# Bringing x to token order without the matrix engine: VectorE block transposes and DMA copies in a fused state-space and feed-forward kernel

## The reference

```python
# state-space layer: d_inner 1024, 8 heads of 128, state 64, convolution over 4 positions
zxbcdt = u @ W_in.T                         # z | x, B, C | dt
xBC = silu(conv_b + sum(xp[:, k:k+l] * conv_w[:, k] for k in range(4)))
dt = softplus(dt + dt_bias);  A = -exp(A_log)
# per chunk of positions and head: L = exp(segment sums of dt*A), lower triangle
Y_diag = einsum(C, B, L, x*dt)              # inside the chunk
states = einsum(B, decay, x*dt)             # what the chunk adds to the state
Y_off  = einsum(C, state before the chunk, exp(cum))
y  = Y_diag + Y_off + x * D
yg = y * silu(z)
out = (yg * rsqrt(mean(yg*yg) + eps) * norm_w) @ W_out.T
x1 = layernorm(u + out)                     # layernorm without scale or shift
# feed-forward: W_q = clip(round(W/mean|W|), -1, 1) * mean|W|
h  = silu(x1 @ Wup_q.T) * (x1 @ Wgate_q.T)  # 2048 hidden units
x2 = layernorm(x1 + h @ Wdown_q.T)
```

## Time and profile before

| | |
|---|---|
| three timed runs, us | 1473.92, 1475.54, 1475.65; median 1475.54 |
| profiled execution, us | 1476.25, its span 1473.3 |
| granted TensorE clock | 0.995 of 2.4 GHz over the span |
| busy | PE 98%, VectorE 69%, ScalarE 58%, GpSimd 29% |
| state-space part | start to 785 us |
| first 512 tokens of the feed-forward part | 785 to 875 us |
| 56 pairs | 875 us to the end, 10.36 us each |

### The profile page before, as it was taken

How to read it: one execution, slowest core, us unless ns; L and a number is a source line. 1 busy time by engine, 2 the same in 40 slices (tenths; PEclk the granted TensorE clock), 3 DMA queues, 4 the chain that set the end, 5 groups by cost and what they waited for, 6 DMA issues and landing times.

```text
span 1473.3 us, 26856 instructions
## 1 busy us (share of the span) xinstructions
PE 1444.9 (98%) x10132; PEld 1300.4 (88%) x10132; DVE 1021.8 (69%) x2223; ACT 857.7 (58%) x1651; POOL 430.6 (29%) x540
## 2 busy tenths in 40 slices
PE   8999999999999999999998999999999999999997
PEld 8889898889898898988977889999999999999996
DVE  6876686667766776677668987766665666666555
ACT  7877667676765766766762234545445454545443
POOL 5334454445435453454362106500000000000000
PEclk9999999999999999999999999999999999999999
DMA  7113312332233232322247333545353545445341
GB/s 272 65 58 87 101 59 73 87 101 86 65 96 87 83 91 57 101 88 59 87 136 253 110 110 128 167 139 161 108 179 101 158 129 162 134 127 163 94 136 65
DMA packets 141760, 168.05 MB, mean 114 GB/s; under 512 B 76480, under 2 KB 85184, under 8 KB 141632
## 3 DMA queue, kind: packets, MB, share of 16 engines
q1 hardware_dynamic: 141632, 166.35, 36.8%
HBM read 132.62 MB, written 33.69 MB: 113 GB/s over the span
## 4 chain that ended last, share of the span: by engine, by line
PE 86%; DMA 4%; DVE 4%; ACT 2%; issue 2%; SPq 1%; POOL 0%; POOLq 0%; DVEq 0%; ACTq 0%
PE ps L403 25%; PE ps L265 21%; PE ps L473 16%; PE ps L359 11%; PE ps L393 3%; PE ps L313 3%; DMA x_scratch<-s_rr 3%; PE ps L321 2%; PE ps L330 1%; PE ps L300 1%; DVE s_xact L827 1%; SPq L1376 1%; DMA s_bcx<-ct_scratch 1%; PE ps L233 1%; DVE s_rr L974 0%
## 5 line engine op out<-in xcount | busy, mean ns | idle before, releaser
L403 PE MATMUL ps<-s_xoh,s_S 128*128 128x256 f32 x896 | 220.4, 282 | 0.1
L403 PE MATMUL ps<-s_xol,s_S 128*128 128x256 f32 x896 | 220.3, 282 | 0.0
L473 PE MATMUL ps<-s_tern,s_hl 128*128 128x512 f32 x504 | 199.2, 395 | 0.0
L473 PE MATMUL ps<-s_tern,s_hh 128*128 128x512 f32 x504 | 199.2, 395 | 0.0
L265 PE MATMUL ps<-s_uhi,s_whi 128*128 128x256 f32 x1088 | 179.8, 287 | 3.0 <-ACT s_uhi L543 3.0
L403 PEld LDWEIGHTS ps<-s_xoh,s_S 128*128 128x128 f32 x896 | 169.5, 189 | 5.9 <-issue 0.8
L265 PE MATMUL ps<-s_ulo,s_whi 128*128 128x256 f32 x1088 | 173.6, 282 | 0.3 <-DVE s_ulo L812 0.3
L403 PEld LDWEIGHTS ps<-s_xol,s_S 128*128 128x128 f32 x896 | 169.5, 189 | 4.8
L265 PE MATMUL ps<-s_uhi,s_wlo 128*128 128x256 f32 x1088 | 173.5, 282 | 0.0
L1267 POOL TENSOR_TENSOR s_lnb<-s_lnb,s_cst 128x1 f32<-128x1 f32 x32 | 18.9, 595 | 501.2 <-DVE s_lnb L1115 501.2
L403 PE MATMUL ps<-s_xol,s_tern 128*128 128x256 f32 x672 | 163.7, 281 | 0.0
(11 more groups left out here) (178 smaller groups left out, 2985.8 us busy)
## 6 DMA issues: line engine op xcount, KB each, us to landing
s_S<-wsum_scratch SPq DMA_DIRECT2D x48, 512.0 KB, 3.6
s_S<-wsum_scratch SPq DMA_DIRECT2D x96, 256.0 KB, 3.4
s_bcx<-ct_scratch SPq DMA_DIRECT2D x32, 512.0 KB, 3.8
s_wst<-in_wffn SPq DMA_DIRECT2D x48, 256.0 KB, 2.8
s_wraw<-in_wffn SPq DMA_DIRECT2D x16, 768.0 KB, 7.8
s_uraw<-in_uT SPq DMA_DIRECT2D x16, 512.0 KB, 6.2
s_rr<-in_un SPq DMA_DIRECT2D x32, 256.0 KB, 3.1
x_scratch<-s_rr SPq DMA_DIRECT2D x32, 256.0 KB, 2.2
```

The source lines that it names most:

```text
L403: o = e.matmul(bank[:, 256 * mi:256 * mi + 256], wt(mi, k), xo[g % 2][:, x, k, :], start=(first and mi == 0 and k == 0 and xo is xoh), sto ...
L473: o = e.matmul(DB[c][:], y[:, 128 * c:128 * c + 128], tern[:, j, 1024:1536], start=(j == 0 and lo == 0), stop=(j == 15 and lo == 1))
```

## The change

What it does:

- `TR` and `f_xTe` are gone, and with them 256 instructions on PE and 64 on ScalarE. `f_xtr(n, k)` on VectorE transposes each block of 32 x 32 of an x tile in place in `xact`, one instruction of [128, 2, 256] a tile, 64 in all.
- `load_xT(c)` on SP's queue moves the blocks to their places: 16 DMAs a chunk, each from 32 partitions of `xact` to 32 partitions of `xT`, 8 heads by 32 numbers, so pieces of 128 B. 512 such DMAs in all.
- Y, `f_xw` and `f_xe` of the next group wait for these DMAs (`xT_landed`). `B0` is now Y's alone.
- `f_x1` moves from VectorE to ScalarE, as scale and bias of one activation; GpSimd's `f_rs1` computes the bias in a second instruction on one column.
- Only chunks 0 to 11 are transposed by `f_xt` and stored by `store_xt` in the state-space part. For chunks 12 to 31 x1 is read back from DRAM (`load_xr`), transposed (`f_xt2`) and stored (`store_xt2`) in the pairs Q of the feed-forward part, one chunk in each odd Q below 40.
- The lists that set the order are written anew on all engines, also those that say which engine splits which weight tile at the start.

```diff
-        def TR(c, half):
-            n = c // 2
-            w.wait_ge(s_silc, 5 * n + 5)
-            if c % 2:
-                w.wait_ge(s_xTe[half], c)
-            elif c:
-                w.wait_ge(s_gate[half], c)
-            for i in range(4):
-                o = e.transpose(B0[half][:, 128 * i:128 * i + 128],
-                                xact[:, 4 * half + i, 128 * (c % 2):128 * (c % 2) + 128], ident)
-            o.then_inc(s_TR[half], 1)
...
+    def xT_landed(w, c):
+        w.wait_ge(d_xT[c % 3], 256 * (c // 3 + 1))
...
         def Y(c):
             w.wait_ge(s_DI, c + 1)
-            later = c + 1 if c % 2 else c + 2
+            xT_landed(w, c)
             for half in range(2):
-                w.wait_ge(s_xTe[half], later)
-                if c % 2:
-                    w.wait_ge(s_gate[half], c)
+                w.wait_ge(s_gate[half], c)
...
# ScalarE: f_xe(n, k), the first writer of xact
-                w.wait_ge(s_TR[0], 2 * n)
-                w.wait_ge(s_TR[1], 2 * n)
+                for c in range(2 * n - 2, 2 * n):
+                    if c >= 0:
+                        xT_landed(w, c)
...
-        def f_xTe(c, half):
-            w.wait_ge(s_TR[half], c + 1)
-            if c >= 3:
-                w.wait_ge(s_Y, c - 2)
-                w.wait_ge(s_xw, c - 2)
-            e.activation(xT[:, c % 3, 4 * half:4 * half + 4, :].rearrange("p h s -> p (h s)"),
-                         B0[half][:], AF.Copy).then_inc(s_xTe[half], 1)
...
+        def f_x1(c):
+            v, r = lnb[:, c % 2, :], rr[:, c % 3, :]
+            w.wait_ge(s_rs1, 2 * c + 2)
+            e.activation(r, r, AF.Identity, scale=v[:, 11:12], bias=v[:, 12:13]).then_inc(s_x1, 1)
...
# VectorE
+        def f_xtr(n, k):
+            w.wait_ge(s_silc, 5 * n + k + 1)
+            x = xact[:, 2 * k - 2:2 * k, 0:256]
+            e.transpose(x, x).then_inc(s_xtr, 1)
...
-        def f_x1(c):
-            v, r = lnb[:, c % 2, :], rr[:, c % 3, :]
-            w.wait_ge(s_rs1, c + 1)
-            e.tensor_scalar(r, r, v[:, 8:9], v[:, 11:12], sub, mult).then_inc(s_x1, 1)
...
+        def f_xt2(c):
+            w.wait_ge(d_xs, 80 * (c - 12) + 16)
+            e.transpose(xtt[:], xtt[:]).then_inc(s_xt, 1)
...
# GpSimd: f_rs1(c)
+            w.wait_ge(s_rs1, 2 * c + 1)
+            e.tensor_scalar(v[:, 12:13], v[:, 8:9], v[:, 11:12], -1.0, mult, mult).then_inc(s_rs1, 1)
...
# SyncE
+        def load_xT(c):
+            w.wait_ge(s_xtr, 4 * (c // 2) + 4)
+            if c >= 3:
+                w.wait_ge(s_Y, c - 2)
+                w.wait_ge(s_xw, c - 2)
+            for i in range(4):
+                t = 128 * (c % 2) + 32 * i
+                for j in range(4):
+                    e.dma_start(xT[32 * i:32 * i + 32, c % 3, :, 32 * j:32 * j + 32],
+                                xact[32 * j:32 * j + 32, :, t:t + 32]).then_inc(d_xT[c % 3], 16)
...
+        def load_xr(c):
+            x1_stored(w, c)
...
+            e.dma_start(xtt[:], x1d[128 * c:128 * c + 128, :]).then_inc(d_xs, 16)
...
# SyncE, one line of the order of a period, before and after
-            load_bc(c + 3); load_wst(3 * n + 3); store_xt(c - 1); load_r0(c + 1); load_wst(3 * n + 4); load_bc(c + 4)
+            store_x1(c - 1); load_wst(3 * n + 2); load_bc(c + 3); load_xT(c + 2); load_r0(c + 1); load_wst(3 * n + 3)
```

More of the change, by code:

```diff
@@ L182, in build_program @@
     U1_AT = 4
[L183 to L187, removed]
+    DVE_LO = [16, 9, 13, 15, 12]
+    WHI_ORDER = [16, 8, 9, 10, 11, 13, 15, 12, 0, 14, 2, 6, 7, 1, 3, 5, 4]
+    POOL_LO = [8, 10, 11, 2, 14, 0, 1, 5, 6, 4, 3, 7]
+    WOHI_ORDER = [2, 3, 0, 1, 7, 4, 5, 6]
+    WOLO_ORDER = [1, 2, 4, 0, 3, 5, 6, 7]
     IP_TILES = [[16], [8, 9], [10, 11], [12, 13], [14, 15], [0, 1], [2, 3], [4, 5], [6, 7]]
@@ L210, in build_program, with x1_count @@
     XQ = ((X11, 0, 0), (D3, 0, 1), (X21, 1, 0), (X22, 1, 1))
+    def xT_landed(w, c):
+        w.wait_ge(d_xT[c % 3], 256 * (c // 3 + 1))
+    def x1_count(c):
+        return sum(80 if i < 12 else 16 for i in range(c % 3, c + 1, 3))
     def x1_stored(w, c):
-        w.wait_ge(d_x1[c % 3], 80 * (c // 3 + 1))
+        w.wait_ge(d_x1[c % 3], x1_count(c))
     def program_pe(e):
@@ L507, in program_pe @@
-        expert(10, 1); down(7); expert(11, 0); expert(11, 1); expert(12, 0); expert(12, 1); down(8); expert(13, 0)
-        expert(13, 1); expert(14, 0); down(9); expert(14, 1); down(10); expert(15, 0); expert(15, 1); down(11)
+        expert(2, 0); expert(2, 1); SQ(c + 1); OP(c + 1); expert(3, 0); expert(3, 1); expert(4, 0); down(0)
+        expert(4, 1); down(1); expert(5, 0); expert(5, 1); down(2); expert(6, 0); expert(6, 1); expert(7, 0)
+        expert(7, 1); down(3); expert(8, 0); down(4); expert(8, 1); expert(9, 0); down(5); down(6); expert(9, 1)
@@ L510, in program_pe @@
+        expert(10, 0); down(7); expert(10, 1); expert(11, 0); down(8); expert(11, 1); expert(12, 0); expert(12, 1)
+        down(9); down(10); expert(13, 0); expert(13, 1); expert(14, 0); expert(14, 1); down(11); expert(15, 0)
+        expert(15, 1)
         for Q in range(56):
@@ L1138, in program_dve @@
+            f_taps(n + 1, 4); f_dd(c + 4); f_GM(n + 1)
+            if m == NG // 2 - 1:
+                wtot()
+            f_xtr(n + 1, 1); f_xtr(n + 1, 2)
+            if m <= 3:
+                f_xt(c)
+            if m == NG // 2 - 1:
+                f_wz(c + 4)
+            f_ms(c + 2); f_gate(c + 3, 0); f_gate(c + 3, 1); f_r1(c + 2); f_sqsum(c + 3); f_xtr(n + 1, 3)
+            f_xtr(n + 1, 4); f_S(c + 3)
             if m < NG // 2 - 1:
@@ L1166, in program_dve @@
                 f_h21(Q - 1); f_h12(Q - 1)
+            if Q % 2 == 1 and Q < 40:
+                f_xt2(12 + Q // 2)
             if p == 2:
@@ L1393, in load_xt @@
             X, kh, h = XQ[i]
-            for c in range(4 * g, 4 * g + 4):
-                x1_stored(w, c)
+            if g < 3:
+                for c in range(4 * g, 4 * g + 4):
+                    x1_stored(w, c)
+            else:
+                w.wait_ge(d_xs, 80 * (4 * g + 2 * h - 10))
             if g == 1:
@@ L1476, in program_sp @@
             e.dma_start(wolr[:, k, :], wout[:, k, :]).then_inc(d_wo[k], 16)
[L1477 to L1478 removed]
+        load_xT(0); load_xT(1); load_wst(2); load_bc(2); load_r0(0); load_bc(3); load_u(3); load_wst(3); load_r0(1)
+        load_xT(2); load_wst(4); store_x1(0); load_xT(3); load_wst(5); store_ct(1); load_wst(6)
         for m in range(1, NG // 2):
             n, c = 2 * m, 4 * m - 2
[L1482 to L1487 removed]
+            load_r0(c); load_bc(c + 2); load_wst(3 * n + 1)
+            if m <= 3:
+                store_xt(c - 2)
+            store_x1(c - 1); load_wst(3 * n + 2); load_bc(c + 3); load_xT(c + 2); load_r0(c + 1); load_wst(3 * n + 3)
+            load_xT(c + 3)
+            if m <= 3:
+                store_xt(c - 1)
+            load_bc(c + 4); load_r0(c + 2); load_bc(c + 5); load_wst(3 * n + 4); load_wst(3 * n + 5)
+            if m < NG // 2 - 1:
+                load_u(n + 2)
+            store_x1(c)
+            if m < NG // 2 - 1:
+                load_u(n + 3)
+            store_x1(c + 1)
+            if m <= 3:
+                store_xt(c)
+            load_xT(c + 4); load_xT(c + 5); store_x1(c + 2)
+            if m <= 3:
+                store_xt(c + 1)
+            if m == NG // 2 - 1:
+                load_xt0()
@@ L1507, in program_sp @@
                 load_xt(g + 1, p - 1)
+            if Q % 2 == 0 and 0 < Q <= 40:
+                store_xt2(11 + Q // 2)
             if Q >= 8:
                 load_ws4(Q)
+            if Q % 2 == 0 and Q < 40:
+                load_xr(12 + Q // 2)
             if p == (4 if g == 1 else 3):
```

194 lines of the change are left out of this document (95 added, 99 removed).

## The result

The changed kernel takes 1529.12 us (median of 4 runs, 1526.45 to 1534.65) against 1475.6: a ratio of 1.0366, 95% interval 1.0332 to 1.0400. It is slower by 53.5 us, where 12 us faster was forecast, and 35 us above the end of the range. A ratio leaves out an execution that ran at a much lower clock throughout; there was one, of e8 (1735.03 us, mean granted clock 0.749).

A forecast was written before the change was run, and what follows sets the result against it. PE was taken as the bound, busy 1444.9 of 1473.3 us. Terms -29 - 2 + 8 + 5.4 + 6 = -11.6 us gave 1464 us; the forecast's own range was 1455 to 1471, the whole range 1444 to 1494 us.

The forecast's parts named there:

- all but the copies: PE's order: transposes removed, -29 us, and half of the repeated wait before the dt projection, -2 us.
- copies, start: Start: nothing queued hides the first group's 32 issues, so PE waits 5.4 us.
- copies, six periods: State-space loop: PE waits for the copy chains, 1.2 us a period, +8 us over 6.5 periods.
- copies, end: End of the state-space part: late copies and r of chunk 29 delay OP(30) and the first expert tile, +6 us.
- the prediction's own price: SP's queue: 480 issues stand on the path once there is a wait, so 0.01 us more per issue costs 4.8 us.
- The issue was mis-sized: SP's queue: one copy's issue taken as 0.64 us, between 0.45 and 0.70, from rows of other shapes.
- rival 2: PE's x tiles: the queue of 32 copies binds the loop from 0.664 us per copy; +17 us, 1493 us, chance 0.28.
- The second half of a period: From Y(c+3): chain of 39.9 us to r's read-out, PE at OP after 39.0, so a 0.9 us wait.
- The transposes, -29 us: PE: 256 transposes at 0.113 us each leave its order, all of it on the path.
- Rival 1: SP's queue: the issue is short, 0.45 us, so no wait in the loop; -31 us, 1444.5 us, chance 0.2.
- Rival 3: VectorE becomes the bound, 1.5 us a period, +10 us: 1474 us, no change, chance 0.12 (with an issue just at 0.66).
- the sign of rival 2: SP's queue: a run of 16 copies taking 11 us or more, where the forecast had 10.2 us.

The follow-up runs named there:

- e8: e7 with a projection tile between the dt projection and its transposes and the low part of u earlier on VectorE: 1520.61 us, 1.0302.
- e1: The changed kernel without the 512 copies, xT holding zeros: 1458.34 us, 0.9878 of the kernel before.
- e7: The changed kernel with VectorE's copy of the cumulative sums moved ahead of the taps of x tile 1: 1522.79 us, 1.0325.
- e4: The kernel before without its 256 PE transposes and ScalarE's 64 copies of them, xT holding zeros: 1460.59 us, 0.9891.
- e13: The changed kernel with the second projection tile moved between the first dt projection and its transposes at the start: 1528.47 us, 1.0374.
- e3: The changed kernel with each copy cut to 4 of its 8 heads, as many issues, half the bytes: 1519.70 us, 1.0294.
- e5: The changed kernel with 8 of a group's 32 copies issued from GpSimd's queue, from group 2 on: 1480.13 us, 1.0026.
- e6: The changed kernel with 16 of a group's 32 copies issued from GpSimd's queue: 1504.56 us, 1.0204.

## Why the prediction was wrong

The sum against e1 and the table (changed minus e1 is what the copies cost, e1 minus before is the rest):

| term | forecast | measured |
|---|---|---|
| all but the copies | -31 | -18 (start +4.0, periods -21.9, end -4.4, feed-forward +4.1) |
| copies, start | +5.4 | +4.3 |
| copies, six periods | +7 | +48.2 |
| copies, end | +7 | +18.4 |

The forecast was 11.6 us less, the spans of the two pages differ by 52.7 us more, a gap of 64 us. As an estimate, by the prediction's own price (4.8 us for each 0.01 us of an issue), the mis-sized issue is 22 us of it. The idle time that the copies brought beyond this is 6 us (48.0 against 19.4 + 22), slower work is 23 us, and 13 us are not the copies'. The first of these used up the gain; without the others the time would have been 1486 us, inside the range.

- **The issue was mis-sized**: 0.64 us taken, 0.687 measured, past the 0.664 at which the gain is used up. From start to start it is 0.65 us in the median, near what was taken; 20 of the 512 issues last 1.1 to 1.9 us, and they make most of the rest. The run of four stores from which the estimate came, 2.57 us, was one of 32 in the trace of before, and one of the shortest; the view of all 128 stores, and the longest run, have the long issues too:

```profile
L1376 SPq DMA_DIRECT2D x1t_scratch<-s_rr x128: 561/628/1631, 112.9 to 873.7; - x128
...
663.02 3.62 SPq L1376 DMA_DIRECT2D x1t_scratch<-s_rr  x4
```

  All 32 runs average 2.70 us, 0.67 us an issue: with this the prediction's own sum gives no gain. The error was inside the bounds, and the text said that the gain hangs on it.
- **The other step that failed is the price of a wait.** Each microsecond that PE waits was counted as one. It is the largest part of what lies beyond 1486 us, and of what lies beyond rival 2's 1493. The mechanism of rival 2 is the one that happened, at its place, but by the two pages 48.0 us idle brought 22.9 us of slower work. The trace of before had one place between the marks that shows it, and it was not looked at: the longest wait of the earlier trace rows, 1.9 us, ends at 564.5, and the windows behind it are:

```profile
564.90:568.20 3.30, 3.30 (x13) 1.79 (x6) 2.23 (x4) 3.25 (x7) 0.05 (x1) 0.50 0.59 110
568.30:571.60 3.30, 3.30 (x16) 2.66 (x15) 2.81 (x7) 0.70 (x2) 1.75 (x2) 1.00 0.00 0
```

- **The second half of a period.** The chain through the copies was the right one, the waiting instruction not: it was not OP but G, which stands earlier in PE's order and whose sums VectorE copies only behind taps that wait for the copies. In the profile Y(c+3) ends at 384.55 and G starts at 420.95, after a wait of 3.26 us: PE was there after 33 us, and the forecast counted on its coming to OP after 39. Moving the copy of the sums ahead (e7) gives 6 us, and leaves the idle time as it was.
- **The transposes, -29 us.** Right as a slot, but "all of it is on PE, which is the path" held only in part: in the old order the removal gives 16 us (e4). In the new order the periods give 21.9 of the 23.7 us that were forecast for them (21.7 and 2), in spite of the new wait of 0.88 us at the dt transposes, which was not seen.
- **Start and feed-forward part.** The new orders cost 4.0 and 4.1 us without any copy, where -3.6 and 0 were counted. In e1's start the clock is at its lower level in two stretches, 13.6 us (first two windows), where the kernel before has none from 10 to 80 us (third):

```profile
12.60:19.40 6.80, 5.97 (x28) 5.98 (x29) 5.68 (x23) 5.04 (x10) 0.00 (x0) 0.50 1.05 395
43.30:50.10 6.80, 5.80 (x25) 5.51 (x26) 5.32 (x12) 6.73 (x9) 0.28 (x1) 0.50 0.00 0
...
10.00:80.00 70.00, 66.68 (x530) 62.46 (x532) 54.61 (x133) 59.49 (x122) 36.29 (x48) 1.00 0.40 143
```

  In the feed-forward part PE waits 2.6 us for a ternary tile, and behind it the clock is at its lower level (0.51 from 871.8 to 875.2); the kernel before waits 0.2 us for such tiles. The row of the changed kernel:

```profile
871.75 0.80 PE L388 MATMUL ps<-s_x1h,s_tern 128*128 128x512 f32 x1 [2.59 <-DVE s_tern L997]
```

  Why the clock falls at the start is left open (e13), and the second was not tried.
- **End.** The copies cost 18.4 us instead of 7. The marks of the six periods end before the last period, so its waits are in here, and the clock. By the windows over this part PE is idle 16.6 us against 5.9 in e1, and busy 7.7 us longer (119.5 against 111.8), with 20.5 us at half the clock where e1 has none.
- **Rivals.** Rival 1 could not have happened even with free copies, which give 1458 us and not 1444.5. Rival 3 (VectorE) did not: with the same VectorE order and fewer copies the waits go.
- **Signs.** PE's busy time did not fall by 29 us. Of the 16 runs of 16 copies seven took 11 us or more, the sign of rival 2, and all took over 10.2. The feed-forward part is 4.1 us longer, past the 2 us that the prediction named as a sign of being wrong.
- Of the sentences on the Trainium skill's page "DMA: Bandwidth & Descriptors": the copies in pieces of 128 B landed 2.0 us after issue (median), about the 1.8 that was forecast, and half the bytes changed little. So no sign of the penalty for small pieces is seen here, which agrees with its section on small descriptors for copies inside SBUF; no run has larger pieces to compare.

## What to carry to other kernels

Where many small DMAs replace work on the bounding engine, multiply their number on one queue by the issue time and see whether that product stands in a loop through the buffer they free; if it does, the number of issues is the cost, not the bytes. Split them over two queues before anything else, and give the second engine no more than its own work allows: 8 of 32 on GpSimd gave back 49 us, 16 of 32 only 25. Size an issue by all of its kind in a trace, not by one run.

Count a wait of PE of some microseconds at more than its length, since the products behind it may run at half the clock. How much more isn't fixed. Against e1, with the same instructions on PE, by the pages:

| | PE idle more, us | PE busy more, us | busy for each us idle |
|---|---|---|---|
| changed | 48.0 | 22.9 | 0.48 |
| e3 | 41.0 | 18.2 | 0.44 |
| e7 | 44.8 | 17.5 | 0.39 |
| e5 | 17.1 | 7.1 | 0.42 |
| e6 | 37.7 | 8.5 | 0.23 |

In e6 one wait of 12.6 us holds a third of the idle time.

## What was not expected of the hardware

- An issue of a copy [32, 8, 32] inside SBUF takes 0.61 us on SyncE's queue in the median, a [32, 4, 32] 0.60, but a [32, 8, 32] takes 0.687 in the mean of all runs, with the gaps and the long ones; on GpSimd's queue 0.58 to 0.59 in a run, and there the engine itself is busy with it.
- Of the 11 waits of PE of 1.7 us or more that the changed kernel has in the six periods, 8 were followed by a stretch at 1.2 GHz (1.8 to 4.0 us of wait), three were not (1.7, 1.9 and 2.2 us), and none of the shorter ones was. In e7 a wait of 2.95 us was not followed by one (the window 461.9 to 466.0 has 1.00), and one of 1.66 us was (214.0 to 218.2, 0.60). What decides is not settled by these runs.
